# Marks for the dense half of a graph pass: one column at a time as a per-partition scalar, where four were compared with a broadcast column

## The chip, the cores and the metric

The kernel runs on one core of one Trainium2 chip. The metric is the device time of one execution in microseconds (us), so lower is better. About 0.2% of it (8 us) is what a measurement of this kernel can tell from no change.

## The reference

A graph network of 6,250 nodes with 128 features and 106,250 edges (random pairs in both directions and one loop per node, sorted by destination). Its message passing, cut to what matters:

```python
h = relu(layernorm(x))
deg = segment_sum(1, dst) + 1;  dinv = rsqrt(deg)
h  = segment_sum((h @ W1)[src] * dinv[src] * dinv[dst], dst) + b1      # first pass over the edges
h  = h / max(norm(h), 1e-12)
ev  = sigmoid(h[src] @ We1[:H] + h[dst] @ We1[H:] + be1)
na  = relu(segment_sum(ev * h[src], dst) @ Wn1 + bn1)                  # second pass
ev2 = sigmoid(na[src] @ We2[:H] + na[dst] @ We2[H:] + be2)
g   = relu(segment_sum(ev2 * na[src], dst) @ Wn1 + bn1)                # third pass
out = segment_sum((g @ W2)[src] * dinv2[src] * ev2 * dinv2[dst], dst) + b2   # fourth pass
x = x + out
```

## The kernel before

There are four passes over the edges. An edge tile is 128 edges, one to a partition. In the **first pass** all 832 edge tiles are gathered: GpSimd (POOL) issues one indirect DMA for each tile (line 567), which brings the source rows of 128 edges from a table in HBM into one of 16 places of `rows`. SyncE (lines 462 to 468) waits for each landing, passes it on to TensorE as `tiles_landed`, waits until TensorE is done with an older tile, and gives the place back to GpSimd as `slots_free`. An edge tile and a node tile (128 nodes) that share edges make a **pair**; there are 880, taken in 220 **quads** of four. For each quad VectorE makes four one-hot matrices at once (`weigh`, line 1402), TensorE multiplies each with its gathered rows (`multiply`, line 974), and VectorE adds the four results to the accumulator of their node tile (`add`, line 1410).

The three later passes don't gather all edges. For one half of the edge tiles (the *dense half*) they use a matrix of **counts**: how many edges lead from node to node. It is made during the first pass, beside its pairs. The edges of the dense half are laid out in 816 **slots** (416 edge tiles and 400 windows of 8 destination nodes, laid over one another in a staircase). For each slot VectorE makes two matrices of zeros and ones, the **marks**: `lo_hot` (128 columns: which of 128 source nodes in its tile) and `cell_hot` (392 columns: which of 8 destinations by 49 source tiles). TensorE clears a region of PSUM with a matmul of zeros (line 988), multiplies the two marks into it (line 993), and ScalarE (ACT) copies each finished region out as 16-bit counts (line 715). After each 16 slots ScalarE sends one tile of counts, 1,568 KB, to HBM (the **flush**, line 729), 51 times in all.

The marks are made for four slots at a time by `mark(b)`, for b from 0 to 203, with two VectorE instructions. Each compares a row of 16-bit column numbers (`cell_no`: 0 to 391, its first 128 for `lo_hot`), repeated four times, with four columns of `lo_col` or `cell_col` (16-bit; a column holds for each of the 128 edges of a slot which number is to be marked), each repeated along its row. The marks lie in a ring of three (`LM_RING`). `hots_ready` tells TensorE that a block of four is there; `cells_done` tells VectorE that a ring place is free again.

The order is written out by hand. On TensorE quad q is: `multiply(q)`, then `count(b)` for the block that falls on it. On VectorE it is: `weigh(q + 1)`, four `add`s of q, then `mark(b + 1)`. Blocks fall on quads 10 to 215 by `quads_before`, one to a quad except for two quads without one. Every 16 pairs and every 16 slots TensorE, ScalarE and VectorE read the next 16 or 32 addresses into their registers (lines 348 and 354); these are the `TENSOR_LOAD` rows.

The columns are made once, ahead of the first pass, from PSUM (lines 1351 and 1355), and `cell_no` is copied from a table of numbers (line 1347). Ring, columns and numbers share the big buffer `tab_area` with the tables of the other passes.

## Time and profile before

| what | us |
| --- | --- |
| time, median of 3 runs (3939.12 to 3944.6) | 3939.19 |
| the profiled execution, its own time | 3923.9 |
| its span, first to last instruction | 3922.1 |
| TensorE busy in it | 3301.8 |
| VectorE busy | 2512.9 |
| GpSimd busy | 2516.7 |
| ScalarE busy | 1476.3 |
| first pass, from the first gather to the last added pair | about 122 to 1501 |
| of it with marks | 224 to 1485 |

The first pass takes a third of the span. The mean granted clock of TensorE is 0.807 of full speed over the span. The marks are 503.6 us of VectorE's busy time (204 x 685 ns and 204 x 1784 ns).

How to read it: PE is TensorE's matmuls, PEld its weight loads, DVE is VectorE, ACT ScalarE, POOL GpSimd, SP SyncE; a q behind a name is that engine's sequencer. A busy share says how long an engine had something in it, not whether anyone waited for that. That is read from who ended an engine's idle time ("<-"), and "issue" there is time in which the engine waited for nothing that the profile shows. Line numbers are those of the listing.

### The profile page before, as it was taken

The page shows a single profiled execution, that of the slowest core. Times are in us where ns is not written, and L with a number is a line of the kernel's source. Part 1 is how long each engine was busy: PE and PEld are TensorE (multiplying, and loading weights), DVE is VectorE, ACT ScalarE, POOL GpSimd, SP SyncE. Part 2 cuts the span into 40 slices and gives each one's busy share as a digit, 9 for nine tenths or more (in the row PEclk, how much of TensorE's full clock was granted, in tenths as well). Part 3 has the DMA queues.
Part 4 walks back from the last instruction along what each step waited for, and adds up shares of the span by engine and source line. Part 5 has one row for each costly group of instructions (what it writes and reads, how often), then busy time and mean ns, then how long its engine had stood idle before and what let it go on. Part 6 is the DMA issues. An engine that isn't in the chain of part 4 may idle for free.

```text
span 3922.1 us, 57417 instructions
## 1 busy us (share of the span) xinstructions
PE 3301.8 (84%) x14640; PEld 2445.8 (62%) x14640; DVE 2512.9 (64%) x6096; ACT 1476.3 (38%) x3026; POOL 2516.7 (64%) x2280
## 2 busy tenths in 40 slices
PE   0668888888888886799999998999999996777776
PEld 0434444444444444688888886888888875666665
DVE  5646666666666665566666665666666655666667
ACT  6013333333333333444444444444444452223332
POOL 5477777778888884566666624666666407776773
PEclk9955555555555557899999999999999998899998
DMA  4223332333333334444444423444444334333333
GB/s 108 60 75 105 106 104 96 101 106 108 107 107 109 113 113 128 131 138 138 133 133 139 127 89 105 128 136 139 125 139 139 110 97 127 93 113 104 103 104 98
DMA packets 215571, 444.33 MB, mean 113 GB/s; under 512 B 42815, under 2 KB 156563, under 8 KB 208716
## 3 DMA queue, kind: packets, MB, share of 16 engines
q0 software_dynamic: 81664, 195.50, 18.0%
q10 hardware_dynamic: 93063, 210.70, 15.6%
q1 hardware_dynamic: 40549, 34.68, 3.0%
q8 instruction: 127, 2.08, 0.2%
q14 instruction: 168, 1.38, 0.1%
HBM read 326.44 MB, written 105.37 MB: 110 GB/s over the span
## 4 chain that ended last, share of the span: by engine, by line
PE 77%; issue 9%; DVE 8%; another core or an unknown queue 2%; DMA 1%; ACTq 1%; POOL 1%; SPq 0%; DVEq 0%; ACT 0%; POOLq 0%
PE ps L1028 26%; PE ps_high L1020 13%; PE ps L974 9%; PE ps_high L988 9%; PE ps_high L993 9%; PE ps_high L1028 6%; DVE acc L1484 2%; PE ps L1104 2%; DVE tab_area L1467 1%; DVE weights L1460 1%; DMA counts<-tab_area 1%; PE ps_high L1094 1%; ACTq L737 1%; DVE acc L1467 1%
## 5 line engine op out<-in xcount | busy, mean ns | idle before, releaser
L567 POOL DMA_INDIRECT rows<-table,edge_src x1248 | 1319.7, 1057 | 731.4 <-SPq L468 446.5
L1028 PE MATMUL ps<-tab_area,acc 128*128 128x256 f32 (+2 forms) x5880 | 1238.4, 355 | 99.8 <-DVE acc L1484 62.3
L567 POOL DMA_INDIRECT rows<-table,acc x832 | 1064.3, 1279 | 321.8 <-issue 209.6
L1028 PEld LDWEIGHTS ps<-tab_area,acc 128*128 128x128 f32 x5880 | 1001.9, 195 | 244.0 <-DVE acc L1484 84.3
L1020 PE MATMUL ps_high<-rows,weights 128*128 x2784 | 660.7, 353 | 125.3 <-issue 60.2
L715 ACT ACTIVATE tab_area<-ps_high x816 | 405.8, 497 | 914.0 <-PE ps_high L993 513.0
L1467 DVE TENSOR_TENSOR acc<-acc,ps_high 128x256 f32 (+1 forms) x938 | 394.1, 420 | 510.7 <-PE ps_high L1020 428.1
L803 ACT ACTIVATE step<-xbuf,rows 128x128 f32 x928 | 362.7, 394 | 752.5 <-PE ps_high L1020 563.4
L1020 PEld LDWEIGHTS ps_high<-rows,weights 128*128 128x128 f32 x2784 | 490.0, 195 | 196.1 <-issue 87.6
L1484 DVE TENSOR_TENSOR acc<-acc 128x640 f32<-128x640 f32 x735 | 601.6, 819 | 10.6 <-DMA tab_area<-tab_area 6.7
L1410 DVE TENSOR_TENSOR acc<-acc,ps 128x128 f32 x880 | 253.4, 288 | 446.4 <-PE ps L974 303.5
L988 PE MATMUL ps_high<-acc 1*128 1x392 f16 x816 | 409.8, 502 | 121.2 <-issue 102.9
L974 PE MATMUL ps<-rows,weights 128*128 x1760 | 432.4, 426 | 90.5 <-issue 77.4
L974 PEld LDWEIGHTS ps<-rows,weights 128*128 128x128 f32 x1760 | 410.3, 327 | 118.6 <-issue 108.9
L812 ACT ACTIVATE acc<-xbuf,tab_area 128x640 f32 x490 | 399.8, 816 | 55.8 <-PE ps_high L1028 51.9
L993 PE MATMUL ps_high<-tab_area 128*128 128x392 f16 x816 | 412.9, 506 | 0.0
L1028 PE MATMUL ps_high<-tab_area,acc 128*128 128x256 f32 (+2 forms) x1470 | 393.7, 350 | 0.0
L812 ACT ACTIVATE acc<-xbuf,source 128x640 f32 x245 | 200.2, 827 | 461.3 <-PE ps_high L1028 286.8
L1423 DVE TENSOR_TENSOR tab_area<-tab_area 128x1568 f16<-128x1568 f16 x204 | 364.0, 1784 | 0.0
L988 PEld LDWEIGHTS ps_high<-acc 1*128 1x128 f16 x816 | 80.1, 98 | 376.4 <-issue 251.0
L1028 PEld LDWEIGHTS ps_high<-tab_area,acc 128*128 128x128 f32 x1470 | 265.9, 195 | 27.7 <-DVE acc L1467 1.3
L1467 DVE TENSOR_TENSOR tab_area<-tab_area,ps_high 128x128 f32 x469 | 133.1, 284 | 231.5 <-PE ps_high L1020 147.8
(231 smaller groups left out, 1990.6 us busy)
## 6 DMA issues: line engine op xcount, KB each, us to landing
acc<-counts ACTq DMA_DIRECT2D x105, 1120.0 KB
counts<-tab_area ACTq DMA_DIRECT2D x51, 1568.0 KB
rows<-table,edge_src POOLq DMA_INDIRECT x1248
rows<-table,acc POOLq DMA_INDIRECT x832
table<-tab_area SPq DMA_DIRECT2D x12, 903.0 KB, 4.7
acc<-xbuf ACTq DMA_DIRECT2D x1, 6400.0 KB, 26.9
table<-acc SPq DMA_DIRECT2D x7, 448.0 KB
table<-tab_area SPq DMA_DIRECT2D x6, 448.0 KB, 3.0
```

Of the source, the lines that this page charges most:

```text
L567: nc.gpsimd.indirect_dma_start(rows[:, t % UNROLL, 0:row_floats[k]], None, tables[k], bass.IndirectOffsetOnAxis(ap=index[:, t:t + 1], axis ...
L715: ins = act.activation(c_cells[:, bass.ds(count_at[m % UNROLL], NODE_TILES, step=PART // WINDOW), :], ps_high[:, bass.ds(done_at[m % UNROL ...
L803: ins = act.activation(gates[:, m % G_RING, :], xbuf[:, bass.ds(node, 1), :].rearrange("p o f -> p (o f)"), ACT.Sigmoid, bias=rows[:, bass ...
L812: ins = act.activation(gate_blocks[:, n % S_RING, :], xbuf[:, bass.ds(low + GROUP_TILES * (it // NODE_TILES), GROUP_TILES), :].rearrange(" ...
L974: ins = nc.tensor.matmul(ps[m % QUAD][:, 0:FEAT], weights[:, m % (2 * QUAD), :], rows[:, bass.ds(first_pass.slots[u], 1), 0:FEAT].rearrang ...
L988: ins = nc.tensor.matmul(ps_high[:, bass.ds(first_pass.zero_at[u], CELLS)], no_cells[:, 0:PART], no_cells[:, 0:CELLS], start=True, stop=Tr ...
L993: nc.tensor.matmul(ps_high[:, bass.ds(first_pass.cell_at[u], CELLS)], lo_hot[r][:, m % QUAD, :], cell_hot[r][:, m % QUAD, :], start=False, ...
L1020: nc.tensor.matmul(ps[DENSE_BANKS + m % PAIR_BANKS][:, 0:WIDTH[k]], weights[:, m % W_RING, :], rows[:, bass.ds(known["slots"][m % UNROLL], ...
L1028: ins = nc.tensor.matmul(ps[j][:, 0:WIDTH[k]], gate_blocks[:, n % S_RING, j * PART:(j + 1) * PART], table[:, h, 0:WIDTH[k]], start=(h == 0 ...
L1423: nc.vector.tensor_tensor(cell_hot[b % LM_RING], cell_no.unsqueeze(1).to_broadcast([PART, QUAD, CELLS]), cell_col[:, at].unsqueeze(2).to_b ...
L1467: ins = nc.vector.tensor_tensor(sums, sums, ps[bank][:, 0:WIDTH[k]], ALU.add)
L1484: nc.vector.tensor_tensor(block, block, count_in[n // CHUNK % 2][:, :, n % CHUNK, :], ALU.mult)._wait_ge(gated, n + 1).then_inc(blocks_rea ...
```

## The change

`mark(b)` no longer makes two instructions for four slots but eight: for each slot one comparison of the 128 numbers with the slot's column of `lo_col`, and one of the 392 numbers with its column of `cell_col`. The column is now a per-partition scalar of the instruction and not a second tensor. Numbers and marks stay 16-bit. `lo_col` and `cell_col` are 32-bit now, so they take twice the room, and `tab_area` grows from 13,568 to 14,400 words. The same marks are made, at the same place in VectorE's order, with the same waits and one signal to TensorE, behind the eighth.

```diff
-        tab_area = sb("tab_area", [PART, 13568])
+        tab_area = sb("tab_area", [PART, 14400])
...
-        lo_col, cell_col = (within(tab_area, at_cols + k * (SLOTS // 2), [SLOTS], f16) for k in range(2))
-        cell_no = within(tab_area, at_cols + SLOTS, [CELLS], f16)
+        lo_col, cell_col = (within(tab_area, at_cols + k * SLOTS, [SLOTS]) for k in range(2))
+        cell_no = within(tab_area, at_cols + 2 * SLOTS, [CELLS], f16)
...
-                    at = slice(b * QUAD, (b + 1) * QUAD)
-                    nc.vector.tensor_tensor(lo_hot[b % LM_RING], cell_no[:, 0:PART].unsqueeze(1).to_broadcast([PART, QUAD, PART]),
-                                            lo_col[:, at].unsqueeze(2).to_broadcast([PART, QUAD, PART]), ALU.is_equal)
-                    nc.vector.tensor_tensor(cell_hot[b % LM_RING], cell_no.unsqueeze(1).to_broadcast([PART, QUAD, CELLS]),
-                                            cell_col[:, at].unsqueeze(2).to_broadcast([PART, QUAD, CELLS]), ALU.is_equal).then_inc(hots_ready, 1)
+                    for m in range(b * QUAD, (b + 1) * QUAD):
+                        nc.vector.tensor_scalar(lo_hot[b % LM_RING][:, m % QUAD, :], cell_no[:, 0:PART], lo_col[:, m:m + 1], None, ALU.is_equal)
+                        ins = nc.vector.tensor_scalar(cell_hot[b % LM_RING][:, m % QUAD, :], cell_no, cell_col[:, m:m + 1], None, ALU.is_equal)
+                    ins.then_inc(hots_ready, 1)
```

On VectorE, between the last `add` of a quad (line 1410) and the next `weigh` (line 1402), this stands in the place of the first block of marks. The rows are those of the difference, of before with a minus and of the change with a plus; the ISA rows are the waits of the `add`s.

```order
 L1410 ISA
 L1410 TENSOR_TENSOR acc1<-acc1,ps3 128x128
-L1421 TENSOR_TENSOR tab_area<-tab_area 128x512
-L1423 TENSOR_TENSOR tab_area<-tab_area 128x1568
-L1402 TENSOR_TENSOR weights<-iota,acc2 128x512
```

```order
+L1421 TENSOR_SCALAR tab_area<-tab_area 128x128
+L1422 TENSOR_SCALAR tab_area<-tab_area 128x392
+L1421 TENSOR_SCALAR tab_area<-tab_area 128x128
+L1422 TENSOR_SCALAR tab_area<-tab_area 128x392
+L1421 TENSOR_SCALAR tab_area<-tab_area 128x128
+L1422 TENSOR_SCALAR tab_area<-tab_area 128x392
+L1421 TENSOR_SCALAR tab_area<-tab_area 128x128
+L1422 TENSOR_SCALAR tab_area<-tab_area 128x392
+L1402 TENSOR_TENSOR weights<-iota,acc2 128x512
```

Two rows became eight, 2,080 columns in both; what stands ahead of them and behind is the same. This happens 204 times: VectorE has 1,224 rows more. No other engine's rows change.

Ahead of the first pass, where VectorE takes the columns from PSUM, one kind of row changes, since the result now has the type of the source:

```order
 L1351 TENSOR_SCALAR tab_area<-ps3 128x204
-L1355 CAST tab_area<-ps0 128x204
-L1355 CAST tab_area<-ps1 128x204
-L1355 CAST tab_area<-ps2 128x204
-L1355 CAST tab_area<-ps3 128x204
+L1355 COPY tab_area<-ps0 128x204
+L1355 COPY tab_area<-ps1 128x204
+L1355 COPY tab_area<-ps2 128x204
+L1355 COPY tab_area<-ps3 128x204
```

Nothing moved there; four casts are four copies.

## Rows read from the trace of the kernel before

**Rows 1.** Stretches: us, busy of PE, PEld, DVE, ACT, POOL, clock, DMA share, GB/s

```profile
260.00:860.00 600.00, 505.21 (x1523) 248.15 (x1523) 387.49 (x665) 190.45 (x383) 471.90 (x358) 0.50 0.31 102
936.00:1460.00 524.00, 460.82 (x1391) 226.86 (x1390) 351.74 (x608) 172.57 (x347) 424.11 (x328) 0.50 0.32 109
```

**Rows 2.** Timeline of one quad: start us, us, engine, line [idle before <-releaser]

```profile
799.89 1.91 PE L974 MATMUL ps<-rows,weights 128*128 x8
...
800.67 1.57 DVE L1410 TENSOR_TENSOR acc<-acc,ps 128x128 f32 x4 [0.73 <-PE ps L974]
...
802.15 0.68 DVE L1421 TENSOR_TENSOR tab_area<-tab_area 128x512 f16<-128x512 f16 x1
...
802.76 1.78 DVE L1423 TENSOR_TENSOR tab_area<-tab_area 128x1568 f16<-128x1568 f16 x1
...
802.97 2.40 POOL L567 DMA_INDIRECT rows<-table,acc  x1 [0.30 <-issue]
...
804.46 0.68 DVE L1402 TENSOR_TENSOR weights<-iota,acc 128x512 f32<-128x512 f32 x1
...
805.09 1.91 PE L974 MATMUL ps<-rows,weights 128*128 x8
```

**Rows 3.** Who TensorE waited for, 260 to 860 us: us, times, longest

```profile
PE ps_high L988 <- issue: 47.2, 18, 4.0
PE ps L974 <- issue: 32.8, 24, 1.4
```

**Rows 4.** The same, 936 to 1460 us

```profile
PE ps L974 <- issue: 15.4, 21, 0.8
PE ps L974 <- DVE weights L1402: 0.7, 1, 0.7
```

**Rows 5.** Timeline behind one flush, and TensorE's address loads there (ns, starts)

```profile
608.81 0.35 ACTq L729 DMA_DIRECT2D counts<-tab_area  x1
...
614.16 2.14 ACT L715 ACTIVATE tab_area<-ps_high  x4 [5.71 <-DMA counts<-tab_area]
...
L348 PEldq TENSOR_LOAD <-acc x2: 1102/1102/1103, 615.4 to 616.5; - x2
...
617.88 2.07 PE L974 MATMUL ps<-rows,weights 128*128 x8 [1.36 <-issue]
```

**Rows 6.** SyncE's queue, 600 to 1400 us: who it waited for

```profile
SPq L468 <- PE ps L974: 621.2, 384, 8.8
SPq L465 <- DMA rows<-table,acc: 6.5, 3, 3.1
```

**Rows 7.** Groups on GpSimd, 300 to 1450 us: xcount | busy us, mean ns | idle

```profile
L567 POOL DMA_INDIRECT rows<-table,acc x704 | 921.4, 1309 | 229.7 <-issue 177.1 <-SPq L468 52.6
```

**Rows 8.** Line by line, VectorE: ns min/median/max, first and last start; and a timeline row

```profile
L1335 DVE TENSOR_SCALAR acc<-acc x4: 635/637/640, 119.6 to 124.6; 104x816 f32<-104x816 f32 x4
...
L1342 DVE TENSOR_SCALAR xbuf<-acc x4: 460/461/519, 126.8 to 130.7; 104x464 f32<-104x464 f32 x4
...
L1309 DVE TENSOR_SCALAR tab_area<-tab_area,node_base x7: 278/278/279, 112.6 to 113.7; 128x128 f32<-128x128 int32 x7
...
112.57 1.46 DVE L1309 TENSOR_SCALAR tab_area<-tab_area,node_base 128x128 f32<-128x128 int32 x7
```

**Rows 9.** Timeline of a gather beside the first of a block's two marks

```profile
670.76 0.68 DVE L1421 TENSOR_TENSOR tab_area<-tab_area 128x512 f16<-128x512 f16 x1
671.18 1.08 POOL L567 DMA_INDIRECT rows<-table,acc  x1 [0.30 <-issue]
671.36 1.78 DVE L1423 TENSOR_TENSOR tab_area<-tab_area 128x1568 f16<-128x1568 f16 x1
```

**Rows 10.** Timeline of a gather beside a comparison with a per-partition scalar

```profile
128.70 0.95 POOL L567 DMA_INDIRECT rows<-table,acc  x1 [0.30 <-issue]
129.41 0.46 DVE L1342 TENSOR_SCALAR xbuf<-acc 104x464 f32<-104x464 f32 x1
```

**Rows 11.** Timeline of TensorE at the end of the first pass

```profile
1496.57 0.49 PE L974 MATMUL ps<-rows,weights 128*128 x2 [1.24 <-issue]
```

## Prediction

> **What bounds the kernel now.** I read the stretches of the first pass first, since the change touches no other [rows 1]. TensorE is busy 505 of 600 us in the first and 461 of 524 us in the second, at a granted clock of 0.50, that is at 1.2 GHz. GpSimd is about as full (472 and 424 us), VectorE is not (387 and 352 us). So TensorE or GpSimd bounds the pass, and the next view has to tell which.
>
> The timeline of one quad tells it for TensorE [rows 2]. Its multiplications begin at 799.89 and again at 805.09, and between them there is no gap in it: 5.20 us for each quad, of which four counts take the larger part. VectorE follows: four adds from 800.67, the two marks from 802.15 and 802.76, the next `weigh` from 804.46 to 805.14, and then it is idle for 0.73 us until TensorE's next product. That `weigh` is not for the multiplication at 805.09 but for the one after it, so VectorE is a whole quad ahead.
>
> What TensorE does wait for [rows 3, 4] is no mark. Two waits come back once in 16 slots. One is before the clearing matmul (47.2 us in 18 times): ScalarE, behind a flush, does nothing for 5.71 us [rows 5], so no region of PSUM comes free. The other is before a multiplication (32.8 us in 24 times, 15.4 us in 21 times): its two loads of addresses, 1.10 us each, start at 615.4 and 616.5, end at 617.6, and the multiplication comes at 617.88 [rows 5]. Put together, a period is four quads and both stops: 4 x 5.20 + some 2.5 + 1.36 = 24.7 us. The pass has 51 of them, about 1,260 us. VectorE is named once, with 0.7 us [rows 4].
>
> Is GpSimd late? SyncE sits between it and TensorE. In 800 us it waited 621 us for TensorE and only 6.5 us for a gather to land [rows 6]. So the rows of a gather lie ready when TensorE comes. But GpSimd has little to spare: 704 gathers in 1,150 us took 921.4 us and the idle time before them 229.7 us [rows 7], of which 704 x 0.30 = 211 us is the fixed gap before every gather [rows 2, 10]. That leaves 18 us, or 1.6%.
>
> **What the change does to VectorE.** It removes 204 pairs of instructions. From the start of the first (802.15) to the start of what follows (804.46) a pair takes 2.31 us [rows 2]. It adds eight instructions for each pair. What one costs is not in the trace, since no 16-bit comparison with a per-partition scalar runs there; it is bounded by 32-bit ones. 816 columns take 637 ns and 464 take 461 ns [rows 8], 0.50 ns a column, so they run at two columns a cycle (a mark of today takes 1,784 - 685 = 1,099 ns for 1,056 columns more, one a cycle). Seven in a row with 128 columns take 1.46 us, the last 0.28 us, so they start (1.46 - 0.28) / 6 = 0.197 us apart, although one lasts 278 ns [rows 8]: 0.067 us for the columns and 0.13 us that is fixed. By that a slot costs, for 128 and 392 columns:
> - at one column a cycle: 0.26 + 0.54 = 0.80 us, a block of four 3.2 us (the upper bound);
> - at two: 0.197 + 0.334 = 0.53 us, a block 2.12 us;
> - at four: 0.163 + 0.232 = 0.395 us, a block 1.58 us (the lower bound).
>
> The Trainium skill ("VectorE: DVE Perf Modes", section on the perf-mode tier table) gives such an instruction four results a cycle with 16-bit data in SBUF, and a `tensor_tensor` at most two; the marks of today run at one. By it the last line would be the right one.
>
> I take four, as the numbers and the marks are 16-bit and half the bytes of the 32-bit rows which reach two. VectorE saves 2.31 - 1.58 = 0.73 us a block, 149 us in all; at two columns 0.19 us and 39 us, at one it loses 0.9 us a block.
>
> **What of it lies on the path.** None of the 149 us. Between the start of the marks and the next adds there are 0.60 us of `weigh` (805.14 less the overlap of 0.08, from 804.46), 2.31 us of marks, and idle time: the next adds come 5.20 us after the last, at 805.87. So a block may take 805.87 - 802.15 - 0.60 = 3.1 us without delaying an add. All three bounds lie at or near that, and behind it comes the quad by which VectorE is ahead. Sooner marks only find TensorE still at the block before.
>
> **What it does to GpSimd.** This is where a gain could come from. The gather at 802.97 takes 2.40 us, while others take 0.95 [rows 2, 10]. It ends at 805.37, which is 0.83 us after the second mark does (802.76 + 1.78 = 804.54). The gather at 671.18 fell into the first mark instead, ends at 672.26, again 0.82 us after that one's end (671.44), and is not held by the second mark that had begun at 671.36 [rows 9]. So a gather's first step waits for the end of the one VectorE instruction with two SBUF tensors that runs then, and gets in between two. The mean gather takes 1,309 ns against 950 [rows 7]: 0.36 x 704 / 186 = 1.4 us a block (1,150 of the 1,260 us hold 186 of the 204 blocks). With instructions that start 0.16 to 0.23 us apart a wait is a fraction of that; I take 0.2 us a block. GpSimd gets some 1.1 us a block back, 230 us in all, and will spend them waiting for `slots_free`, because TensorE still frees a place only every 1.38 us.
>
> At the end of the pass TensorE does wait, 1.24 us at 1496.57 [rows 11], for gathers that landed late behind the last flush. With GpSimd a little further ahead I give 1 us of it back, and another 1 us where the marks begin.
>
> Ahead of the pass four casts become copies of the same size, and the longer buffer moves addresses only. I cost both at nothing: they are four of VectorE's instructions, and at the worst 0.1 us each.
>
> **The sum.** 3923.9 (the profiled execution's own time) - 2 = 3921.9. The timed runs lie 15.3 us above the profiled one, so against their median the forecast is 3939.2 - 2 = 3937 us: no difference that a measurement would show (that takes about 0.2%, 8 us).
>
> **Rival 1: GpSimd is held for the whole string (slower).** A comparison at two or more columns a cycle may hold GpSimd off more strongly than today's marks do, so that a gather gets in only when all eight are through. The place is the same gather in each quad; the price is the string's length less the 1.4 us lost now. At 1.58 us this is 0.2 us a block, 37 us on GpSimd, of which it has 20 us to spare: +17 us, 3956. At 2.12 us it is 0.7 us a block, 147 - 20: +127 us, 4066. It decides from a loss of about 1.5 us a block on. Against it: the gather at 128.70 takes 0.95 us, although such a comparison runs from 129.41 to 129.87, over its last 0.24 us, and the comparison is not longer for it either (0.46 us) [rows 10, 8]. And a gather got in between two marks [rows 9].
>
> The Trainium skill ("SBUF — State Buffer", section on who interferes with whom) speaks against this change: a VectorE instruction in a two-port mode takes the port pair that it shares with GpSimd for its whole length, and GpSimd can't write a DMA's descriptors meanwhile, whereas two SBUF inputs hold off its reads alone. By it this rival would be likelier than I make it; the gather at 128.70 shows no such delay.
>
> **Rival 2: TensorE waits for gathers more than the profile says (faster).** The stops before multiplications are put down to "issue". If they are partly late gathers, a freed GpSimd takes away up to 32.8 + 15.4 us and what the rest of the pass has of it, about 50 us: 3889. And the timed runs take 15 us more than the profiled one; if that is GpSimd, which has but 1.6% to spare, running dry, it would go as well: 3924. For it: GpSimd is as full as it can be [rows 7]. Against it: the stops end with the address loads [rows 5], and SyncE hardly ever waited for a landing [rows 6]. If it comes, I expect the 15 us rather than the 50.
>
> **Rival 3: VectorE becomes the bound (slower).** If the eight instructions don't overlap at all, a slot costs, with durations in place of distances and one column a cycle, about 0.35 + 0.63 = 0.98 us, a block 3.9 us. That is 0.8 us more than the 3.1 us of room, so VectorE would take 6.0 us a quad, against 6.1 us that TensorE needs with its stops. It decides from some 4 us a block on. Each 0.1 us beyond costs 204 x 0.1 = 20 us; at 4.1 us the time is 3959. I hold this for unlikely, since seven such instructions in a row do overlap [rows 8].
>
> **How the numbers follow.** The forecast (nothing that can be measured) 0.66; rival 2 0.22 (nearly all of it within 15 to 20 us); rival 1 0.08 and rival 3 0.04. Hence faster by over 0.2% 0.22, within 0.2% 0.66, slower 0.12. The range runs from 3922, which takes in the 15 us of rival 2, to 3956, the lower price of rival 1; the costs that I had to bound don't move it, because all three lie beside TensorE's work.
>
> **What would show it.** In the profile of the changed kernel: the two comparisons start about 0.16 and 0.23 us apart (0.20 and 0.33, or 0.26 and 0.54, by the other bounds), and VectorE's busy time stays near what it was, since durations overlap. The mean gather of the first pass falls from 1.31 towards 1.0 us, GpSimd's idle time on SyncE rises from 53 us to over 200, and TensorE's multiplications still start 5.20 us apart, with the same two stops in a period. Rival 1 would show gathers of 2 us and more and SyncE waiting for landings. Rival 2 would show the stops before multiplications shorter than 1.36 and 0.7 us. Rival 3 would show TensorE waiting for L1422 or for L1402. The forecast is wrong if the stretch from 260 to 1460 us changes its length by over 0.5%.

## The result, and the profile after

| | us |
| --- | --- |
| before, median (3939.12 to 3944.64) | 3941.89 |
| changed, median (3985.46 to 3995.33) | 3993.49 |
| ratio, with its 95% interval | 1.0126 (1.0111 to 1.0140) |
| profiled execution of the changed kernel, its span | 3992.7 |

The change makes the kernel 1.3% slower, some 50 us, although everything that it was meant to do to VectorE happened. One string of marks in the changed kernel, from the timeline (start us, us, engine, line):

```profile
943.49 0.25 DVE L1421 TENSOR_SCALAR tab_area<-tab_area 128x128 f16<-128x128 f16 x1
943.65 0.35 DVE L1422 TENSOR_SCALAR tab_area<-tab_area 128x392 f16<-128x392 f16 x1
943.93 0.24 DVE L1421 TENSOR_SCALAR tab_area<-tab_area 128x128 f16<-128x128 f16 x1
...
945.11 0.68 DVE L1402 TENSOR_TENSOR weights<-iota,acc 128x512 f32<-128x512 f32 x1
```

The next instruction starts 0.16 us behind the start of a short comparison (128 columns) and 0.23 to 0.28 us behind that of a long one (392), and the block takes 945.11 - 943.49 = 1.62 us where it took 2.31 [rows 2].

The same two stretches as in [rows 1], changed kernel (us, busy of PE, PEld, DVE, ACT, POOL, clock, DMA share, GB/s):

```profile
260.00:860.00 600.00, 489.26 (x1472) 240.10 (x1472) 316.12 (x1196) 182.90 (x368) 341.57 (x349) 0.50 0.30 100
936.00:1460.00 524.00, 437.15 (x1317) 214.64 (x1316) 280.43 (x1069) 164.31 (x331) 305.70 (x311) 0.50 0.31 104
```

The clock is the same. GpSimd is busy 342 us in place of 472, and TensorE does less in the same time: 1,472 matmuls in place of 1,523, then 1,317 in place of 1,391. So the pass itself runs 3 to 5% slower. Its last multiplication shows by how much: it starts at 1500.0 us before (first row) and at 1555.9 after (second row; ns min/median/max, first and last start).

```profile
L974 PE MATMUL ps<-rows,weights x1760: 275/421/583, 173.0 to 1500.0; 128*128 x196
```

```profile
L974 PE MATMUL ps<-rows,weights x1760: 274/421/582, 172.8 to 1555.9; 128*128 x196
```

These 55.9 us are the loss (the timed medians differ by 51.6). From there to the end of the span it is 2422.1 us before and 2436.8 us after; but the kernels below take 2424 to 2443 us there as well, in stages whose code is the same, and the one that differs least from before (e4) 2442. So the profiled execution of before was probably short in these stages, by the 15 us by which its timed runs were longer than it.

**Where TensorE stands.** The clearing matmuls from 300 to 1450 us, in the kernel before:

```profile
L988 PE MATMUL ps_high<-acc 1*128 1x392 f16 x745 | 374.1, 502 | 111.0 <-issue 94.1 <-ACT tab_area L715 16.9
```

The same in the changed kernel, and its GpSimd row, which answers to [rows 7]:

```profile
L988 PE MATMUL ps_high<-acc 1*128 1x392 f16 x709 | 355.6, 501 | 154.2 <-issue 70.7 <-ACT tab_area L715 54.4 <-DVE tab_area L1422 29.1
...
L567 POOL DMA_INDIRECT rows<-table,acc x673 | 662.0, 984 | 486.5 <-SPq L468 323.6 <-issue 162.9
```

Before each clearing TensorE stood still for 111.0 / 745 = 0.149 us on average, and now for 154.2 / 709 = 0.217 us. Over the whole pass its idle time before L988 is 121.2 us in the kernel before and 171.1 us in the changed one, and before the multiplications (L974) it is 90.5 and 97.0 us. So 50 of the 56 us sit in front of L988 and 6 in front of L974. It is not a longer wait for a flush alone. In the second half of the pass the kernel before has one stop a period before a clearing, such as this:

```profile
1013.34 0.50 PE L988 MATMUL ps_high<-acc 1*128 1x392 f16 x1 [2.12 <-issue]
```

At the same place the changed kernel has two, and between them a longer stop before the multiplications (1.71 us, where the kernel before has 0.82 us at 1009.15 us):

```profile
1016.43 0.50 PE L988 MATMUL ps_high<-acc 1*128 1x392 f16 x1 [1.94 <-issue]
1019.08 2.07 PE L974 MATMUL ps<-rows,weights 128*128 x8 [1.71 <-issue]
1023.07 0.50 PE L988 MATMUL ps_high<-acc 1*128 1x392 f16 x1 [1.92 <-issue]
```

**What is new: TensorE's signals come late.** The timeline of the changed kernel around one of those places, 695 to 700 us:

```profile
695.78 0.51 PE L993 MATMUL ps_high<-tab_area 128*128 128x392 f16 x1
...
697.20 0.50 ACT L715 ACTIVATE tab_area<-ps_high  x1 [1.15 <-PE ps_high L993]
697.35 0.94 POOL L567 DMA_INDIRECT rows<-table,acc  x1 [0.31 <-issue]
...
697.82 1.92 PE L974 MATMUL ps<-rows,weights 128*128 x8
...
700.05 0.50 ACT L715 ACTIVATE tab_area<-ps_high  x1 [2.35 <-remote]
...
700.14 1.25 DVE L1410 TENSOR_TENSOR acc<-acc,ps 128x128 f32 x4 [2.92 <-PE ps L974]
700.30 0.94 POOL L567 DMA_INDIRECT rows<-table,acc  x1 [2.01 <-SPq L468]
```

The multiplications of the quad start at 697.82. In [rows 2] the first `add` comes 0.78 us behind them; here it comes 2.32 us behind. ScalarE's copies resume at 700.05, VectorE at 700.14 and GpSimd, whose places are freed by the same signals, at 700.30. Three engines that wait for nothing in common but TensorE start within 0.25 us. The times at which the trace has the semaphores change say the same: the signals of the two counts that started at 696.65 and 697.52 stand at 699.92 and 699.96, and the four of this quad at 700.01, 700.05, 700.09 and 700.13. They are 0.04 us apart, where the four pairs of matmuls that they report start 0.43 us apart. So the signals were held back and came in one string. Late work behind matmuls that started on time would not fit that, though the ends of matmuls are only modelled in this profile.

Two signs of this are counted in each trace, from 260 us to the end of the first pass. A **late add** is a quad whose eight multiplications follow one another without a stop and whose first `add` starts over 1.2 us behind the first of them (0.78 us is the usual distance). **Late copies** are a row of ScalarE's copies that start over 1.5 us behind the start of their count (0.65 us is usual), those within 9 us behind a flush left out. The kernel before has none of either; the changed kernel has 26 late adds, about one in two periods, and 49 rows of late copies, about one in each. A late copy frees its region late, and TensorE can stand still for that at L988 ("<-ACT tab_area L715", 16.9 us before and 54.4 us now). The new "<-DVE L1422" (13 times) is no sign of the loss: it stands behind a late add in about half of its cases, and e16 below, which has no loss, names the marks there 15 times (34.4 us). Neither count gives the size of a loss, as the runs below show.

### The profile page after: what moved, and what is told of

Read it like the earlier page. It is cut to its first block, busy times and chain, and to the rows that moved or that the text cites. A ratio compares the mean times of both kernels' runs of the same rounds, so it can differ in the third digit from the quotient of the medians.

```text
span 3992.7 us, 58641 instructions
## 1 busy us (share of the span) xinstructions
PE 3314.3 (83%) x14640; PEld 2461.3 (62%) x14640; DVE 2381.5 (60%) x7320; ACT 1475.2 (37%) x3026; POOL 2269.1 (57%) x2280
## 4 chain that ended last, share of the span: by engine, by line
PE 75%; DVE 9%; issue 8%; another core or an unknown queue 2%; ACTq 2%; DMA 1%; ACT 1%; POOL 1%; DVEq 1%; SPq 0%; POOLq 0%
PE ps L1028 26%; PE ps_high L1020 13%; PE ps L974 9%; PE ps_high L993 9%; PE ps_high L988 8%; PE ps_high L1028 6%; DVE acc L1483 2%; PE ps L1104 2%; ACTq L354 1%; DVE tab_area L1466 1%; DVE weights L1459 1%; DMA counts<-tab_area 1%; DVE acc L1466 1%; ACTq L737 1%
## 5 line engine op out<-in xcount | busy, mean ns | idle before, releaser
L567 POOL DMA_INDIRECT rows<-table,edge_src x1248 | 1317.6, 1056 | 749.0 <-SPq L468 373.5
L567 POOL DMA_INDIRECT rows<-table,acc x832 | 819.0, 984 | 621.0 <-SPq L468 404.1
L1028 PEld LDWEIGHTS ps<-tab_area,acc 128*128 128x128 f32 x5880 | 1013.6, 198 | 235.7 <-DVE acc L1483 90.9
L715 ACT ACTIVATE tab_area<-ps_high x816 | 405.6, 497 | 972.7 <-PE ps_high L993 462.7
L988 PE MATMUL ps_high<-acc 1*128 1x392 f16 x816 | 409.3, 502 | 171.1 <-issue 80.3
L974 PE MATMUL ps<-rows,weights 128*128 x1760 | 431.1, 425 | 97.0 <-issue 73.7
L974 PEld LDWEIGHTS ps<-rows,weights 128*128 128x128 f32 x1760 | 409.6, 326 | 124.7 <-issue 111.8
L988 PEld LDWEIGHTS ps_high<-acc 1*128 1x128 f16 x816 | 80.1, 98 | 427.8 <-issue 299.8
L1422 DVE TENSOR_SCALAR tab_area<-tab_area 128x392 f16<-128x392 f16 x816 | 273.1, 335 | 0.0
```

What stands on the lines that cost most here:

```text
L567: nc.gpsimd.indirect_dma_start(rows[:, t % UNROLL, 0:row_floats[k]], None, tables[k], bass.IndirectOffsetOnAxis(ap=index[:, t:t + 1], axis ...
L715: ins = act.activation(c_cells[:, bass.ds(count_at[m % UNROLL], NODE_TILES, step=PART // WINDOW), :], ps_high[:, bass.ds(done_at[m % UNROL ...
L974: ins = nc.tensor.matmul(ps[m % QUAD][:, 0:FEAT], weights[:, m % (2 * QUAD), :], rows[:, bass.ds(first_pass.slots[u], 1), 0:FEAT].rearrang ...
L988: ins = nc.tensor.matmul(ps_high[:, bass.ds(first_pass.zero_at[u], CELLS)], no_cells[:, 0:PART], no_cells[:, 0:CELLS], start=True, stop=Tr ...
L1028: ins = nc.tensor.matmul(ps[j][:, 0:WIDTH[k]], gate_blocks[:, n % S_RING, j * PART:(j + 1) * PART], table[:, h, 0:WIDTH[k]], start=(h == 0 ...
L1422: ins = nc.vector.tensor_scalar(cell_hot[b % LM_RING][:, m % QUAD, :], cell_no, cell_col[:, m:m + 1], None, ALU.is_equal)
```

## The experiments

Two theories were set against each other. **A**: the loss comes over GpSimd. VectorE no longer holds it, and a quick GpSimd somehow delays TensorE. **B**: the loss comes from the new comparisons, their number or their faster mode. A was split up further as it went. One number is worked out for each run: GpSimd's **own time per gather**, which is what it takes without its waits for places: (1150 us - its idle time on SyncE) / gathers, in the stretch 300 to 1450 us. Before: (1150 - 52.6) / 704 = 1.56 us [rows 7]. Changed: (1150 - 323.6) / 673 = 1.23 us. TensorE frees a place every 1150 / 704 = 1.63 us in this stretch.

### Half of the change each

```diff
 e1_lo_scalar: from the kernel before, only the 128-column mark is changed
-tensor_tensor(lo_hot, ...)          +4 x tensor_scalar(lo_hot[m], cell_no[0:128], lo_col[m])
 e2_cell_scalar: only the 392-column mark is changed
-tensor_tensor(cell_hot, ...)        +4 x tensor_scalar(cell_hot[m], cell_no, cell_col[m])
```

> Half of the change: the 128-column mark is made in four comparisons with a per-partition scalar, the 392-column mark stays one broadcast comparison (1.78 us), so GpSimd can still be held by the longer of the two. Theory A (the loss comes because GpSimd is no longer held by VectorE, catches up with the ring of gathered rows and then works at its limit; TensorE's signals are late beside its gathers): GpSimd keeps most of its hold, so most of the loss is absent: 3942 to 3955 us, GpSimd's idle time on SyncE nearer to 53 than to 342 us in the stretch 300 to 1450, under 15 late bursts of TensorE's signals. Theory B (the loss comes from the new instructions themselves: their number, or their faster mode): half the new instructions, about half the loss, 3960 to 3975 us.

> The other half of the change: the 392-column mark is made in four comparisons with a per-partition scalar, the 128-column mark stays one broadcast comparison (0.68 us), so what can hold GpSimd is short. Theory A: GpSimd is nearly as free as in the changed kernel: 3975 to 3995 us, its idle time on SyncE over 200 us, over 30 late bursts. Theory B: half the new instructions, about half the loss, 3960 to 3975 us.

Measured: e1 1.0033 (1.0020 to 1.0046), e2 1.0135 (1.0114 to 1.0157), as slow as the whole change. Late adds: 5 and 30. Both have half of the new instructions, so B's even split fails. What differs is the long broadcast comparison: with it GpSimd's mean gather stays at 1,321 ns, without it it is 1,007 ns. GpSimd's row in e1 and in e2:

```profile
L568 POOL DMA_INDIRECT rows<-table,acc x698 | 921.8, 1321 | 230.1 <-issue 178.8 <-SPq L469 51.4
```

```profile
L568 POOL DMA_INDIRECT rows<-table,acc x675 | 679.6, 1007 | 471.3 <-SPq L469 309.4 <-issue 161.9
```

The small loss of e1 (13 us) has few late signals behind it: 7 rows of late copies, where e2 has 48. GpSimd takes 1.57 us a gather there, and SyncE waits for landings 86 times between 600 and 1400 us, where it did so 3 times [rows 6]:

```profile
SPq L466 <- DMA rows<-table,acc: 147.5, 86, 6.8
```

That these landings cost the 13 us is not shown. TensorE stood still 87.3 us before its multiplications in e1, less than the 90.5 us before, and 138.8 us before its clearings, where it was 121.2 us.

### GpSimd slowed without VectorE, and GpSimd at the end of its ring

```diff
 e3_paced (in the changed kernel, first pass only, after each gather)
+pool.wait_ge(paused, t)
+nc.gpsimd.memset(pause[:, 0:192], 0.0).then_inc(paused, 1)
 e4_before_short (in the kernel before)
-pool.wait_ge(slots_free, t - UNROLL + LAG + 1)
+pool.wait_ge(slots_free, t - UNROLL + LAG + 1 + 3)
```

> The changed kernel, and in the first pass GpSimd also clears a 128 x 192 buffer that nobody uses after each gather (about 0.25 us), which gives back its former pace of one gather in about 1.55 us by other means than VectorE. All of the change's VectorE instructions stay. Theory A: GpSimd waits little for free places again, the late bursts go (under 15) and the time goes back to 3942 to 3955 us. Theory B: nothing on VectorE is different from the changed kernel: 3985 to 4000 us. If GpSimd's added work made it the bound, its idle time on SyncE would be near 0 and TensorE would wait for landings.

> The kernel before with one edit: in the first pass a gather may start only when three more places of the ring are free (it runs at most 12 to 13 tiles ahead instead of 15 to 16), so that GpSimd stands at the ring's limit with the old marks. Theory A, in the form that standing at the limit is enough: the time rises towards 3975 to 3995 us, with over 30 late bursts. Theory B: no instruction of VectorE differs from the kernel before, and a lead of 12 tiles (19 us) is far more than the 2.5 us of a landing: 3938 to 3948 us.

Measured: e3 1.0053 (1.0036 to 1.0069), with an own time of 1.42 us and 18 late adds; e4 1.0004 (0.9995 to 1.0014), 1.55 us, 3 late adds. e3's pause was too short to bring back the 1.55 us that it was meant to, and with 3961 us and 18 late adds it missed what theory A had forecast (3942 to 3955 us, under 15). Even so, giving GpSimd something useless to do takes back over half of the loss, which B can't explain. That GpSimd stands at its limit earlier costs nothing by itself, although SyncE waited for landings 51 times in e4 between 600 and 1400 us.

### More hold, no marks, less hold, pauses in pairs

```diff
 e5_held (changed kernel, ahead of each block of marks)
+tensor_tensor(held[4,256], cell_no[0:256] x4, cell_no[0:256] x4, is_equal)      # used by nobody
 e6_no_marks (kernel before, blocks 3 to 203)
-the two tensor_tensor of mark(b)     +tensor_copy(credit[:, 9:10], ones[:, 0:1])
 e7_weigh_scalar (changed kernel)
-tensor_tensor(weights[4,128], ...)   +4 x tensor_scalar(weights[m], iota, all_pair_dst[m])
 e8_paced_pairs (changed kernel): as e3, but 448 columns, and only after every second gather
```

> The changed kernel with one more VectorE instruction in front of each block of marks: a broadcast comparison of 4 x 256 columns (1.1 to 1.2 us by the 1,784 ns for 1,568 columns) into a buffer that nobody uses. It gives VectorE more work (about 2.8 us a block in front of the adds, still inside its room of 3.1 us) and holds GpSimd again. Theory A (GpSimd no longer held by VectorE is what costs the time): faster than the changed kernel although work was added, 3940 to 3960 us, mean gather of the first pass 1.1 to 1.25 us, GpSimd's idle time on SyncE clearly under the 342 us of the changed kernel. Theory B (the new comparisons themselves cost it): 3990 us or more.

> The kernel before with the marks left out from the fourth block on (TensorE counts with the marks of the first three blocks; a copy of one column takes the place of the two comparisons, so all signals stay). None of the changed kernel's instructions is there, and GpSimd is held by nothing but the making of weights. Theory A: as slow as the changed kernel or slower, 3980 to 4000 us, with the same late signals of TensorE, although VectorE has 500 us less to do. Theory B: no new comparisons, so no loss: 3930 to 3945 us.

> The changed kernel, and the weights of the first pass are made in the same way too: four 128-column 32-bit comparisons with a per-partition scalar in place of the 0.68 us broadcast comparison. It takes away the last VectorE instruction that holds GpSimd in this pass. Theory A, in the form that each bit of hold taken away costs: slower than the changed kernel, 3995 to 4015 us, mean gather 0.95 us. Theory A, in the form that only the phase of the gathers counts: anywhere from 3945 to 4015 us. Theory B: four more instructions a quad, 3998 to 4010 us.

> The changed kernel; after every second gather of the first pass GpSimd clears a 128 x 448 buffer that nobody uses (about 0.6 us), about the same added work as 0.29 us after every gather, but it comes in one piece, so no more than two gathers start 1.25 us apart. If three and more gathers in a row at 1.25 us are what delays TensorE's signals: better than the 3961 us with the pause after every gather, 3940 to 3950 us. If only GpSimd's mean pace counts: the same 3955 to 3965 us. Theory B: 3985 to 4000 us.

Measured: e5 1.0101 (1.0084 to 1.0118), e6 1.0094 (1.0077 to 1.0112), e7 1.0174 (1.0156 to 1.0193), e8 0.9993 (0.9981 to 1.0006). Late adds: 38, 33, 27, 8, in this order (in e5 VectorE's own added comparison can make an add late too). Here theory B falls. e6 has none of the new instructions, and VectorE has some 500 us less to do, yet it is 37 us slower than the kernel before; GpSimd's row of it looks like that of the changed kernel:

```profile
L567 POOL DMA_INDIRECT rows<-table,acc x683 | 660.0, 966 | 491.0 <-SPq L468 320.5 <-issue 170.5
```

And e8 has all of the new instructions, and the loss is gone (3937 us). Its gathers and its pauses:

```profile
L569 POOL DMA_INDIRECT rows<-table,acc x704 | 706.1, 1003 | 272.8 <-issue 136.9 <-SPq L470 135.9
L574 POOL MEMSET pause<- 128x448 f32 x352 | 174.3, 495 | 0.2
```

e7, which takes the last hold away, is the slower for it, at 1.21 us a gather; its 4006 us alone would fit theory B too (3998 to 4010 us). e5 was a weak test: its extra comparison took 695 ns, not the 1.1 to 1.2 us I had worked out, and hardly held GpSimd (mean gather 1,023 ns, own time 1.25 us). It missed its 3940 to 3960 us with 3978.

### How the pause is cut, with and without marks, and the bytes of a gather

```diff
 e9_paced_fours (changed kernel): 928 columns cleared after every fourth gather
 e10_no_marks_pairs: e6 with the pauses of e8
 e11_quarter_rows (changed kernel)
-indirect_dma(rows[:, place, 0:128], table1, index)
+indirect_dma(rows[:, place, 0:32], table1 seen as rows of 32, index)
 e12_short_pauses (changed kernel): 192 columns cleared after every second gather
```

> As the kernel with a pause after every second gather (3937 us), with the same pause in all, but in one piece of about 1.1 us after every fourth gather, so four gathers may start 1.25 us apart. If it is three and more gathers in a row that delay TensorE's signals: 3965 to 3990 us, 15 and more stretches in which ScalarE gets TensorE's signal over 1 us late. If GpSimd's mean pace is all that counts: 3935 to 3945 us, as with pairs.

> The kernel before with the marks left out from the fourth block on (3976 us), and with the pause of 0.5 us on GpSimd after every second gather. If GpSimd's unbroken gathers are the whole cause, with or without marks on VectorE: 3930 to 3942 us. If the loss of the kernel without marks had a cause of its own: 3965 to 3980 us.

> The changed kernel with gathers of the first pass that fetch 32 floats a row in place of 128 (a different row, and the rest of each place holds zeros, so this leaves out three quarters of the bytes and changes what is summed; all instructions, waits and descriptors stay). If what delays TensorE's signals is the data on its way (bytes and landings): few late signals, 3930 to 3950 us. If it is GpSimd's issuing of the gathers, whatever they carry: as slow as the changed kernel, 3980 to 4000 us.

> The changed kernel with a pause of only 0.29 us on GpSimd after every second gather (128 x 192 columns cleared), half of what was added in the kernel with pairs (3937 us) and in the one with a pause after each gather (3961 us). If breaking the run is what counts, however shortly: 3935 to 3945 us. If the added time counts: half way, 3960 to 3975 us.

Measured: e9 0.9988 (0.9977 to 0.9999), e10 0.9999 (0.9988 to 1.0011), e11 1.0138 (1.0115 to 1.0162), e12 1.0058 (1.0036 to 1.0080). I had by then taken three gathers in a row, 1.25 us apart, for the trigger; e9 lets four in a row through and is the quickest of the four, so that theory fell. e10 shows once more that the marks are not needed for the loss nor for its cure. e11 moves a quarter of the bytes and is as slow, so it isn't the traffic of the gathers. e12, with half the pauses, gives back about half. Late adds: 4, 8, 27, 40. So e12 has more of them than the changed kernel and half of its loss: they tell whether signals are held, not what that costs.

### The lead, the rows of a gather, the flush, and the best pace

```diff
 e13_limit (changed kernel): the wait of e4
 e14_half_gathers (changed kernel)
-indirect_dma(rows[0:128, place], ..., index[0:128])   +indirect_dma(rows[0:64, place], ..., index[0:64])
 e15_no_flush (changed kernel)
-dma(counts[tile], c_tiles[:, ring])                   +dma(counts[tile, 0:1, 0:128], c_tiles[0:1, ring, 0:128])
 e16_paced_threes (changed kernel): 832 columns cleared after every third gather
```

> The changed kernel with a shorter lead: a gather of the first pass may start only when three more places of the ring are free. GpSimd's own pace is as in the changed kernel (about 1.25 us a gather with its gap), only the place at which it waits is earlier. If GpSimd's pace between its waits counts: as slow as the changed kernel, 3985 to 4000 us. If it is a ring filled to its last place that counts: 3940 to 3960 us.

> The changed kernel with gathers of the first pass that fetch 64 rows in place of 128 (the other half of each place holds zeros, so this leaves out half of the rows and changes what is summed). Bytes were shown not to matter; this halves the row addresses that GpSimd works through and the rows that land. If the number of rows in a gather counts: fewer than 20 late signals of TensorE and 3940 to 3970 us. If the gathers get shorter and GpSimd's pace is what counts: as slow as the changed kernel or slower, 3990 to 4010 us.

> The changed kernel with flushes that write 256 bytes in place of 1.57 MB (the table of counts is filled with other numbers ahead of the pass, some 100 us, so its total time isn't comparable; this changes what is computed after the pass). It is read from its trace alone: the late signals come once in about 16 slots, as the flushes do. If the flush's traffic takes part in them: under 10 of them in the pass. If not: still 40 or more. In both, ScalarE's stop behind a flush goes.

> The changed kernel with a pause of about 0.8 us on GpSimd after every third gather: about 1.54 us a gather by its own pace, between the kernel with a pause after every fourth gather (1.50 us, 3935 us) and the kernel before (1.58 us, 3940 us), against 1.57 us that TensorE needs. If the own pace is what counts, this lies at or under 3937 us; below the kernel before by over 0.2% would need under 3931 us, which I don't expect.

Measured: e13 1.0117 (1.0101 to 1.0135), e14 1.0183 (1.0164 to 1.0201), e16 0.9968 (0.9958 to 0.9978). e13 has 31 late adds. 18 of them fall on the same quads as in the changed kernel, and in 16 of these 18 GpSimd is three gathers less far: the place in TensorE's program is the same, and a filled ring is not the point. e14's gathers are a little shorter (952 ns), its own time is the lowest of all, 1.19 us, and it is the slowest of all (4018 us, where 3990 to 4010 were forecast for the pace), with 8 late adds but 48 rows of late copies: the number of rows is not the point either. e15 was read from its trace: 42 late adds, more than with the flushes, so the late signals don't need the flush's traffic. e16 was the first to beat the kernel before. Its rows:

```profile
L569 POOL DMA_INDIRECT rows<-table,acc x711 | 720.5, 1013 | 240.1 <-issue 154.9 <-SPq L470 85.2
L574 POOL MEMSET pause<- 128x832 f32 x237 | 192.0, 810 | 0.1
```

That is (1150 - 85.2) / 711 = 1.50 us a gather. It has 1 late add and no late copies, its last multiplication starts at 1492.7 us (1500.0 before), and its time, 3929 us, lies 0.3% under the kernel before. I had not expected it under 3931 us.

### TensorE's own loads, and the pace in single pauses

```diff
 e17_no_slot_loads (changed kernel)
-at = load_slots(TEN, cell_turns, b // 2, ...)     +at = fixed regions in turn, the same in ScalarE's copy
 e18_paced_ones (changed kernel): as e3, but 256 columns
```

> The changed kernel in which TensorE doesn't load the addresses of its counts every 8 slots: it takes fixed ones, in turn, and ScalarE copies from fixed ones too (this changes which sums are counted together). The two loads of the multiplications' addresses every 16 pairs stay. Without the loads TensorE saves up to 1.1 us in 102 places, so its time alone doesn't tell. In the trace: the late signals of the changed kernel stand 2 to 4 slots behind such a load. If the loads take part: under 10 late signals in the pass. If the late signals only stand beside them: 30 or more.

> The changed kernel with a pause of about 0.37 us on GpSimd after every gather: about 1.54 us a gather, the pace of the kernel with a pause after every third gather (3929 us), cut into single pauses. With a shorter pause after every gather (1.46 us a gather) it was 3961 us, while pairs with 1.49 us were 3937 us. If GpSimd's pace alone sets the time: 3925 to 3937 us. If it also counts how the gathers stand to each other: 3945 us or more.

Measured: e17 0.9787 (0.9768 to 0.9805), which can't be compared, since its missing loads save time by themselves; e18 0.9966 (0.9953 to 0.9979; 3914 us where the kernel before took 3927 on the same chip), 2 late adds, own time (1150 - 102.8) / 711 = 1.47 us. e17 has 46 late adds and 41 rows of late copies, and its late adds fall on 18 of the 26 quads of the changed kernel. So the late signals don't need these loads. But TensorE stood still only 26.9 us before its clearings in e17's whole pass, where it was 171.1 us in the changed kernel: what late signals cost hangs on the rest of TensorE's program. e18 shows that the pace counts for more than how the gathers stand to each other: its pauses are single ones, as in e3, only longer.

### All of them in one row

| own time per gather, us | ratio to the kernel before | rows of late copies |
| --- | --- | --- |
| 1.19 half gathers, 1.21 no hold by `weigh` | 1.018, 1.017 | 48, 51 |
| 1.21 no marks, 1.23 the change, 1.23 quarter rows, 1.23 shorter lead | 1.009, 1.013, 1.014, 1.012 | 47, 49, 49, 46 |
| 1.25 half of the change (e2), 1.25 held a little (e5) | 1.014, 1.010 | 48, 42 |
| 1.32 short pauses | 1.006 | 42 |
| 1.42 no marks with pairs, 1.42 a pause each (e3) | 1.000, 1.005 | 5, 10 |
| 1.44 pairs, 1.44 fours | 0.999, 0.999 | 6, 3 |
| 1.47 longer single pauses, 1.50 threes | 0.997, 0.997 | 1, 0 |
| 1.55 before with a shorter lead, 1.56 before | 1.000, 1 | 3, 0 |
| 1.57 half of the change (e1) | 1.003 | 7 |

The late copies are there, 42 to 51 times, in every kernel with an own time of 1.32 us or less, and nearly gone, 10 at most, in every one with 1.42 us or more. The time falls with GpSimd's own time to its lowest at 1.47 to 1.50 us and is a little higher at 1.55 us and above; why is not shown. The gain of e16 and e18 sits before the multiplications, where TensorE stood still 81.6 and 79.2 us in place of 90.5. The own time doesn't order the slow kernels among themselves: e3 lies 21 us above e10, which has the same own time, e5 13 us under e2, and e6 30 us under e7. So something else counts beside the pace.

**What is shown**: the loss comes over GpSimd's pace, whoever sets it, and a quick GpSimd goes with signals of TensorE that are held back; nearly all of the time is lost where TensorE stands before L988. That the held signals make all of these stops is argued, not shown. **What is open**: by what path a quick GpSimd holds the signals. The comparisons, the marks as a whole, the bytes and rows of a gather, the lead, the flush, the grouping of the gathers and TensorE's loads of slot addresses were each taken away or changed, and none of them is it. The other address loads, of TensorE for its multiplications and of ScalarE and VectorE, come once in 16 pairs or slots as well and were left in all runs.

The traces narrow it down. Strings of two or more signals of TensorE under 0.06 us apart occur 54 times in the changed kernel; in 52 of them the first signal stands 2.2 to 2.8 us (the middle one 2.52) behind the start of GpSimd's last gather. That looks like the landing of this gather, whose first record comes 2.23 us behind its start. But with quarter rows (e11) the landings come sooner (2.05 us) and the strings do not (2.50 us). In e12, whose gathers land as in the changed kernel, the middle string comes at 2.16 us, ahead of the first landing. So the strings stand 1.2 to 1.6 us behind the end of GpSimd's last gather, but the landing of that gather alone does not let them go. About a quarter of TensorE's signals have no record in this trace, so some strings may be missed.

## Why the prediction was wrong

It forecast 3937 us (no difference, 0.66) with a range up to 3956; it is 3993.

- **The cost of the new marks: right.** The lower bound, 0.163 + 0.232 us a slot and 1.58 us a block, was taken; measured 0.16, 0.23 to 0.28 and 1.62 us.
- **"None of the 149 us" on the path: right.** VectorE's saved time gave nothing. Its marks are named before L988 now (29.1 us), but e16, which is quicker than the kernel before, has that too (34.4 us).
- **"What it does to GpSimd": right up to its last sentence, and there it failed.** The mean gather fell from 1,309 to 984 ns (expected "towards 1.0 us"), and GpSimd's idle time on SyncE rose from 52.6 to 323.6 us (expected over 200). That it "will spend them waiting for `slots_free`" is what it does. The step that failed is the price of that: nothing. I reasoned only with what GpSimd's work might hand to TensorE sooner, never with what its pace might do to TensorE beside it. It cost 56 us in the pass, 1.4% of the time: TensorE's signals came late in 49 rows of copies where they did in none, and its idle time before the clearing matmuls rose from 121.2 to 171.1 us. The 1.38 us that it gives for a place to come free leaves out TensorE's own stops; over the stretch it was 1.63 us.
- **The -2 us at the ends of the pass: not there**, and of no weight beside the 56.
- **The sum's 15 us between profile and timed runs** I gave in part to GpSimd running dry (rival 2). They lie behind the first pass, in stages that the change doesn't touch.
- **Rival 1 had the sign and nothing else.** No gather was held for a string: gathers became shorter, and SyncE did not wait for one landing between 600 and 1400 us. The Trainium skill ("SBUF — State Buffer", section on who interferes with whom) has a VectorE instruction in a two-port mode keep GpSimd from its descriptors for its whole length; in this case it is the other way round, since the mean gather takes 984 ns with such comparisons (1,005 ns where it runs beside one, 958 ns elsewhere) and 1,309 ns with the broadcast ones.
- **Rivals 2 and 3 did not come.** The stops before multiplications did not get shorter (31.5 us in 23 times against [rows 3]), and VectorE is far from being the bound. A little of rival 2 is in e16 and e18, where late signals are gone and these stops are 9 to 11 us shorter over the pass.
- **The test that I had named worked**: the stretch from 260 to 1460 us held 3 to 5% fewer matmuls, against a bound of 0.5%.

The chance of 0.12 for slower rested on two mechanisms that both needed a *longer* hold of GpSimd. That a *shorter* one could cost was not among the cases, though [rows 7] had the sign that something would move a lot: an engine with 1.6% to spare (4.6%, if its whole idle time on SyncE, 52.6 us, is taken) was to get 20%.

## What to carry to other kernels

An engine that another one holds up may be running at a pace that suits the rest by chance; when a change frees it, its pace is a change of its own, to be priced and tested apart from the instructions that were edited. The cheap test is a useless instruction on the freed engine: if the loss goes with it, the edited instructions did not cost the time, and the pause can even be kept. Here the changed kernel with GpSimd held to 1.47 to 1.50 us a gather (e16, e18) beats both kernels, the one before by 0.3%.

## What the runs showed of the hardware

- TensorE's signals can reach all of their waiters 1.5 us late and together while its matmuls start on time: 2.32 us from the first multiplication to the first add in place of 0.78 us. Their records then stand 0.04 us apart. It happened over 40 times a pass with a GpSimd at 1.32 us a gather or less, and 10 times at most at 1.42 us or more.
- In the changed kernel 52 of 54 such strings come 2.2 to 2.8 us behind the start of GpSimd's last gather, and they come no sooner with gathers that land 0.18 us sooner (e11).
- A 16-bit comparison with a per-partition scalar overlaps with the next one: the next starts 0.16 us behind one of 128 columns and 0.23 us behind one of 392, though they last 0.25 and 0.32 us. The 264 columns more cost 0.07 us, 0.27 ns each; the broadcast marks of before took 1.04 ns for each column more (1,099 ns for 1,056).
- A 16-bit comparison of a row with itself, both repeated four times (e5), took 695 ns for 1,024 columns, 1.5 a nanosecond, where the marks of before, whose second operand is one number repeated along the row, took 1,784 ns for 1,568, or 0.9. Beside it the mean gather was 1,023 ns.
